# Directional convolutions on 128 partitions in six passes of 12 rows

## What is computed

```
xn = group_norm(x)                                # block 0
feat_h, feat_v      = depthwise 1x7 and 7x1 convolution of xn
feat_d45, feat_d135 = depthwise 7x7 convolution whose only taps are a diagonal
context = mean over pixels of feats**2            # 4 x 96 numbers for an image
attn    = softmax over the 4 directions of (leaky_relu(context @ w_att1.T) @ w_att2.T)
x1 = x + conv3x3(sum_d attn[d] * feats[d], w_proj)
out = x1 + L1(group_norm(x1))                     # block 1: softmax linear attention, a real
                                                  # FFT branch, and one 3x3 convolution
```

## Time and profile before

| | |
|---|---|
| times of three runs | 4177.42, 4215.52, 4221.92 us |
| span of the profiled execution | 4236.6 us |
| TensorE busy | 3960.8 us, 93% |
| VectorE busy | 3033.4 us, 72% |
| ScalarE busy | 1695.8 us, 40% |
| GpSimd busy | 209.5 us, 5% |
| mean DMA traffic | 81 GB/s |

### The profile page before, as it was taken

The page is one execution under the profiler, slowest core; times in us unless marked ns, Lnnn a source line. Parts: engine busy times, 40 slices in busy tenths (PEclk is TensorE's granted clock), DMA queues, the critical chain, the costliest instruction groups (busy, mean ns, idle before and its releaser), DMA issues.

```text
span 4236.6 us, 56479 instructions
## 1 busy us (share of the span) xinstructions
PE 3960.8 (93%) x21202; PEld 3254.3 (77%) x21202; DVE 3033.4 (72%) x2829; ACT 1695.8 (40%) x2912; POOL 209.5 (5%) x376
## 2 busy tenths in 40 slices
PE   4659999999999999999999999999999999999998
PEld 2356879968698687968799686986879687896867
DVE  7988877788677878689777876778886887843020
ACT  3413762247412574127622464215641276203430
POOL 1000000100001000000001000010000000010000
PEclk8879799988799799999999877997999979998779
DMA  4372214712155221822147221552218221350002
GB/s 117 88 177 75 61 41 84 188 51 70 29 133 134 52 69 29 202 73 61 41 97 179 56 61 27 126 143 50 71 26 201 74 63 41 76 137 12 1 3 31
DMA packets 164716, 344.11 MB, mean 81 GB/s; under 512 B 110336, under 2 KB 110576, under 8 KB 164432
## 3 DMA queue, kind: packets, MB, share of 16 engines
q1 hardware_dynamic: 141392, 255.36, 24.5%
q0 software_dynamic: 23040, 84.95, 9.1%
HBM read 189.27 MB, written 150.99 MB: 80 GB/s over the span
## 4 chain that ended last, share of the span: by engine, by line
PE 84%; DVE 9%; ACT 3%; issue 3%; DMA 1%; POOL 0%; SPq 0%; DVEq 0%; ACTq 0%; POOLq 0%
PE banks L936 14%; PE banks L937 14%; PE banks L942 14%; PE banks L961 12%; PE banks L951 6%; PE banks L1003 6%; PE banks L967 5%; DVE feat L702 4%; PE banks L968 4%; PE banks L974 3%; PE banks L1013 3%; DVE e_lo L725 2%; PE banks L990 1%; ACT z L529 1%; DMA feat<-feats_d 1%
## 5 line engine op out<-in xcount | busy, mean ns | idle before, releaser
L702 DVE SCALAR_TENSOR_TENSOR feat<-xin,w,feat 96x1536 f32<-96x1536 f32 x540 | 943.6, 1807 | 28.0 <-ACT feat L488 26.9
L936 PE MATMUL banks<-e_hi,a_hi 96*96 96x384 f32 x1728 | 597.7, 346 | 40.9 <-ACT a_hi L572 40.9
L936 PE MATMUL banks<-e_hi,wp_hi 96*96 96x384 f32 x1728 | 587.7, 341 | 24.2 <-DVE x L780 12.1
L961 PEld LDWEIGHTS banks<-mats,z 96*96 96x96 f32 x3072 | 537.8, 259 | 90.2 <-issue 71.0
L937 PE MATMUL banks<-e_lo,a_hi 96*96 96x384 f32 x1728 | 595.2, 345 | 0.0
L937 PE MATMUL banks<-e_lo,wp_hi 96*96 96x384 f32 x1728 | 586.7, 340 | 0.0
L702 DVE SCALAR_TENSOR_TENSOR feat<-xin,wv,feat 96x1536 f32<-96x1536 f32 x288 | 520.7, 1808 | 79.4 <-ACT feat L488 79.4
L702 DVE SCALAR_TENSOR_TENSOR feat<-xin,wh,feat 96x1536 f32<-96x1536 f32 x288 | 520.6, 1808 | 70.1 <-ACT feat L488 69.2
L961 PE MATMUL banks<-mats,z 96*96 96x96 f32 x3072 | 531.5, 347 | 9.8 <-ACT z L529 9.8
L500 ACT ACTIVATE sqjunk<-feat 96x1536 bf16<-96x1536 f32 x192 | 284.1, 1480 | 228.8 <-DVE feat L702 225.5
L563 ACT ACTIVATE res<-banks 96x768 f32<-96x768 f32 x96 | 77.6, 808 | 727.9 <-PE banks L942 727.9
(11 more groups left out here) (145 smaller groups left out, 5261.1 us busy)
## 6 DMA issues: line engine op xcount, KB each, us to landing
feats_d<-feat SPq DMA_DIRECT2D x160, 576.0 KB, 4.1
feat<-feats_d SPq DMA_DIRECT2D x160, 576.0 KB, 6.5
feat<-in_x SPq DMA_DIRECT2D x48, 576.0 KB, 6.9
res<-in_x POOLq DMA_DIRECT2D x96, 288.0 KB, 4.0
out<-x POOLq DMA_DIRECT2D x96, 288.0 KB, 2.8
out<-res POOLq DMA_DIRECT2D x96, 288.0 KB, 4.4
xin<-in_x SPq DMA_DIRECT2D x32, 792.0 KB, 9.1
xin<-in_x SPq DMA_DIRECT2D x16, 684.0 KB, 10.1
```

The source lines that it names most:

```text
L702: dve.scalar_tensor_tensor(out=dst, in0=src, scalar=taps_w[d](k), in1=dst, op0=ALU.mult, op1=ALU.add).then_inc(tap_done, 1)
L936: pe.matmul(dst, whi[:, t, :], rows(e_hi, a0, n, dx), start=(t == CENTRE_FIRST[0]), stop=False)
L961: last = pe.matmul(ps[0:H, c * W:(c + 1) * W], z[:, :, 4 * g + c], w_dft, start=(c == 0), stop=(c == 3), skip_group_check=True)
```

## The change

- Chunks have 12 rows; `products`, `fg_high`, `fg_low` and the statistics of x run in 8 chunks instead of 6.
- The directional convolutions use all 128 partitions in six passes. Partitions 0 to 95 take chunks 5 to 0, one in each pass. Partitions 96 to 127 take 32 of the 96 channels of chunk 7 in each of passes 0 to 2, and of chunk 6 in passes 3 to 5 (`extra`). The instructions of `taps`, `first_tap` and `square` become 128 x 1152 in place of 96 x 1536, and are as many as before.
- Weights, norm parameters and sums of squares exist in three variants, one for each third of the channels (`wt`, `xpar`, `sqx`, `att1x`). `hidden` has 16 matmul calls in place of 4, of which 12 read 32 rows from partition 96; the group sums of x have 4 calls in place of 1.
- Each pass is loaded with two DMAs and stored with two for each direction (one in pass 5, where chunk 0 stays). Four more loads of x in `start` and eight more loads from `feats_d` for an image.
- The zeroing of edge rows moves from VectorE (`edge_rows`) to ScalarE (`norm_chunk`, one activation with scale 0 in four of the six passes).
- In image 0 `last_direction` has 18 groups of 7 matmul calls with 128 x 128 diagonals (21 of them, made by ScalarE at the start) in place of 24 groups of 7 with 96 x 96. The diagonals lie where `e_hi` and `e_lo` lie later, so GpSimd zeroes the pads only when `last_direction` is done.
- `SUMS_AFTER` becomes (0, 0, 0, 0, 0, 1, 1, 1). Statistics of x go over 24 pieces of 384 in place of 18 of 512.

```
-CR = 16
+LANES = 128
+CR = 12
+PASSES = 6
+VARIANTS = 3
+QUAD = LANES - C
-SUMS_AFTER = (0, 0, 0, 1, 1, 1)
+SUMS_AFTER = (0, 0, 0, 0, 0, 1, 1, 1)
+def extra(q):
+    return q % VARIANTS, NCH - 1 - q // VARIANTS
...
-        xin = sb("xin", [C, 2, XR, XP])
-        feat = sb("feat", [C, DIRS, CR * W])
+        xin = sb("xin", [LANES, 2, XR, XP])
+        feat = sb("feat", [LANES, DIRS, CR * W])
...
+                v, ch = extra(q)
+                lo, hi, at = rows_of(ch)
+                sp.dma_start(xin[C:LANES, q % 2, at:at + hi - lo, PAD:PAD + W],
+                             x[v * QUAD:(v + 1) * QUAD, lo * W:hi * W].rearrange("c (r w) -> c r w", w=W))\
+                    .then_inc(xin_loaded[q % 2], 16)
...
-                        sp.dma_start(feats_d[d, :, ch * CR * W:(ch + 1) * CR * W], feat[:, d]).then_inc(feat_stored[d], 16)
+                        sp.dma_start(feats_d[d, v * QUAD:(v + 1) * QUAD, xch * CR * W:(xch + 1) * CR * W],
+                                     feat[C:LANES, d]).then_inc(feat_stored[d], 16)
+                        if q < PASSES - 1:
+                            sp.dma_start(feats_d[d, :, ch * CR * W:(ch + 1) * CR * W], feat[0:C, d])\
+                                .then_inc(feat_stored[d], 16)
...
                     if not second:
+                        pool.wait_ge(last_dir_sums, VARIANTS * PASSES)
                         zero_pads()
...
+                act.activation(all_rows, all_rows, ACT.Identity, scale=xpar[:, v, 0:1], bias=xpar[:, v, 1:2])\
+                    .then_inc(xin_normed, 1)
+                act.wait_ge(xin_normed, b * (VARIANTS + 1) + min(q, VARIANTS) + 1)
+                act.activation(outside, outside, ACT.Identity, scale=0.0).then_inc(xin_ready, 1)
...
-                                dve.wait_ge(fin_ready, (b - 1) * NG + min(NG, 2 * ch + 3))
+                                dve.wait_ge(fin_ready, (b - 1) * NG + min(NG, (ch + 1) * CR // GR + 1))
...
+                for v in range(VARIANTS):
+                    last = pe.matmul(small_ps[C:LANES, 494 + 2 * v:496 + 2 * v], group[:, v * QUAD:(v + 1) * QUAD], mv[:],
+                                     start=True, stop=True)
...
+                    for v in range(VARIANTS):
+                        for d in range(DIRS):
+                            at = (v * DIRS + d) * MID
+                            last = pe.matmul(small_ps[0:MID, 504:505], att1x[:, at:at + MID], sqx[C:LANES, v, d:d + 1],
+                                             start=False, stop=(v == VARIANTS - 1 and d == DIRS - 1))
```

More of the change, by code:

```diff
@@ L46 @@
 STATS = N // BANK
-XSTAT = CR * W // BANK
+XPIECE = 384
+XSTATS = N // XPIECE
+XSTAT = CR * W // XPIECE
+STORES = 2 * PASSES - 1
 U_MAX = 2 * STATS
@@ L103, in taps_before @@
 def taps_before(b):
-    return 0 if first_image(b) else b * (NCH * TAPS) - NCH * (KT - 1)
+    return 0 if first_image(b) else b * (PASSES * TAPS) - PASSES * (KT - 1)
 def unit_taps(b, u, k, parity):
@@ L116, in firsts_before @@
 def firsts_before(b, q):
[L118 removed]
+    return q * (DIRS - 1) if first_image(b) else b * (DIRS * PASSES) - PASSES + q * DIRS
 def tap_shift(d, k):
@@ L393, in start @@
             def start(b):
-                gn_pow(gnx_small, GN_SMALL, b, 5, 0, gnx_pow)
+                wait(pool, gnx_small, b * GN_SMALL + 5)
+                pool.tensor_tensor(xgp[:, 1], xgp[:, 1], half[:], ALU.pow).then_inc(gnx_pow, 1)
             def step(b, first, second, more):
@@ L441, in _ @@
             pool.wait_ge(consts_set, 5)
+            pool.memset(half[:], -0.5).then_inc(consts_set, 1)
+            pool.wait_ge(consts_set, 6)
             steps(pool, start, step)
@@ L805, in products @@
                 flat = acc[:].rearrange("p r c -> p (r c)")
-                part = feat[:, summed(ch, 0)]
+                part = feat[0:C, summed(ch, 0)]
                 for k in range(k0, k1):
@@ L831, in start @@
             def start(b, between=lambda: None):
-                for n in range(STATS):
+                for n in range(XSTATS):
                     x_stats(b, n, n + 1)
-                    if n % (2 * XSTAT) == 2 * XSTAT - 1 and n + 1 < STATS:
+                    if n % 8 == 7 and n + 1 < XSTATS:
                         between()
@@ L1072, in hidden @@
                     for d in range(DIRS):
-                        last = pe.matmul(small_ps[0:MID, 504:505], att1[:, d, :], l0v[:, d:d + 1], start=(d == 0),
-                                         stop=(d == DIRS - 1))
+                        pe.matmul(small_ps[0:MID, 504:505], att1[:, d, :], l0v[:, d:d + 1], start=(d == 0), stop=False)
+                    for v in range(VARIANTS):
+                        for d in range(DIRS):
+                            at = (v * DIRS + d) * MID
+                            last = pe.matmul(small_ps[0:MID, 504:505], att1x[:, at:at + MID], sqx[C:LANES, v, d:d + 1],
+                                             start=False, stop=(v == VARIANTS - 1 and d == DIRS - 1))
                     last.then_inc(l0_ps, 1)
```

217 lines of the change are left out of this document (120 added, 97 removed).

## The result

The changed kernel takes 4347.7 us (median of 4 runs, 4310.22 to 4358.38), the kernel before 4218.72 us in the same set (4 runs, 4177.42 to 4255.25): a ratio of 1.0324, with an interval of 1.0214 to 1.0433. That is 129 us slower, where 4207 us and no change were forecast. The profiled execution has a span of 4336.8 us with a mean granted clock of 0.867, against 4236.6 us with 0.906.

A forecast was written before the change was run, and what follows sets the result against it. TensorE's work and clock were taken to bound seven of eight rounds. Span 4236.6 - 34 (image 0) + 25 (seven other images) = 4228 us, so a time of about 4207 us; range 4150 to 4262 us.

The forecast's parts named there:

- Taps of image 0 and start: Image 0: 108 shorter VectorE taps save 43 us; later loads at the start cost 1.5 us, `hidden` 2 us.
- rival (5): Taps of image 0: 128 lanes take as long as 96 x 1536 did, the 43 us are gone; 4250 us, chance 0.03.
- Product phase of image 0: Image 0's product phase: eight chunks waiting for their loads take 71.3 us instead of 65.7, so +5.6 us.
- `hidden`: The `a` convolution of the other seven images: 24 more TensorE instructions of `hidden` cost +1.3 us an image.
- rival (3): TensorE: 32-row and 32-column matmuls drain it four times an image, 1.5 us an image; 4217 us, chance 0.10.
- Stall at block 2: The `wp` convolution of seven images: block 2 waits for the later x1_sum(0), 2.5 us an image, between 0 and 7.
- rival (2): The `wp` convolution stalls the full 7 us in seven images, plus 2 to 3 us low clock; 4259 us, chance 0.15.
- The sum of these: Whole kernel: image 0 gains 34 us, the other seven images lose 3.6 us each, 25 us in all.
- rival (4): All eight images: the clock alone can move their sum by 25 us to either side; chance 0.05, in favour.
- the prediction's own bound of 4.9: Seven images: from a loss of 4.9 us an image on, they outweigh the 34 us gained in image 0.
- A count: SyncE queue: 28 more DMA issues for stores and loads of features, taken as having cover.

The follow-up runs named there:

- e9: The changed kernel with each first-pass DFT matmul writing its product twice, 192 columns instead of 96: 4137.7 us, ratio 0.9763.
- e10: The kernel before with each first-pass DFT matmul writing its product twice, 192 columns instead of 96: 4135.96 us, ratio 0.9759.
- e3: The kernel before with ScalarE's unit work placed four uses earlier and nothing added: 4228.59 us, ratio 1.0121.
- e4: The changed kernel plus one ScalarE operation of 0.83 us in the rows stage, on data nobody reads: 4259.78 us, ratio 1.0185.
- e2: The changed kernel without the 12 matmul calls of `hidden` that read 32 rows from partition 96: 4291.28 us, ratio 1.0238.
- e7: The kernel before with the x1 sums as late as the changed kernel has them: 4255.3 us, ratio 1.0142.
- e5: The changed kernel with the same DFT matmuls in a more even order of short and long ones: 4240.19 us, ratio 1.0106.
- e6: The kernel before with the same DFT matmuls in a more even order of short and long ones: 4263.36 us, ratio 1.0205.
- e8: The changed kernel with the even DFT order and four x1 sums between the chunks, one chunk earlier: 4176.26 us, ratio 0.9961.
- e1: The changed kernel with x1_sum(0), (1), (2) each one chunk earlier: 4302.24 us, ratio 1.0246.
- e12: The changed kernel with four x1 sums between the chunks, one chunk earlier, DFT stages as they were: 4272.28 us, ratio 1.0055.
- e11: The changed kernel with doubled columns in the first-pass DFT matmuls and four x1 sums, one chunk earlier: 4103.61 us, ratio 0.9688.

## Why the prediction was wrong

Its terms, one by one:

- *Taps of image 0 and start*, -43.3 + 1.5 + 2 = -39.8 us: measured -38.6: -44.3 from the first tap to the end of the squares, +3.7 for the start (40.58 us instead of 36.89) and +2.0 for `hidden` and what follows it. The start was taken at 1.5 within 0 to 5, and the taps gave 1 us more than forecast. Lanes are free (1.410 us a tap, forecast 1.41), so rival (5) falls. First `maxes` at 352.8 us, forecast 351.
- *Product phase of image 0*: 70.1 us, forecast 71.3. The `wp` convolution there ran longer at the low clock behind a wait of 20.9 us, so the step cost more in the end: -38.6 + 4.4 + 2.2 = -32.0 us, forecast -34.
- *`hidden`*: timeline of TensorE after, around it, in image 1:

```profile
686.73 0.52 PE L1113 MATMUL banks<-l0v,att 96*48 96x1 f32 x8
687.18 1.23 PE L1117 MATMUL banks<-sqx,mats 32*48 32x1 f32 x24
688.35 0.42 PE L972 MATMUL banks<-e_hi,a_hi 96*96 96x384 f32 x1
...
689.65 0.52 PE L972 MATMUL banks<-e_hi,a_hi 96*96 96x384 f32 x1
```

  From 686.73 to 688.35 us, 1.62 us for 32 instructions where 0.44 us went for 8; forecast 1.8. The 24 of them take 1.17 us, 0.049 us each. TensorE drains nowhere that these rows show: the drain at a change of mode, which the Trainium skill states (TensorEngine Tiling (Array Packing), Key Properties), isn't borne out by them, and rival (3) falls. What was left out: a microsecond later the convolution runs at 1.2 GHz for some 3 us (a matmul 0.52 us instead of 0.34). With it, the `a` convolution is 2.5 us longer an image, forecast 1.6.
- *Stall at block 2*: 2.9 us an image, forecast 2.5, and x1_sum(0) 20.3 us behind the copy of block 11, forecast 18 to 21. But the `wp` convolution grew by 5.4 us, since TensorE is at the low clock for 4 to 12 us of it, before 3 to 5. The prediction had priced this in rival (2), for a stall of 7 us, and not for its own of 2.5.
- *The sum of these*: with the clock held up (e9 against e10), after is 34.0 us earlier at the first `maxes` (351.2 against 385.2) and 37.0 us slower over the seven rounds (5.3 us each, forecast 3.6), +3.8 us from profile to profile and +1.7 between the medians, where -9 was forecast. The forecast of this part was 11 to 13 us off, and came that near partly by luck: in e9 against e10 the two convolutions cost 8.7 us an image, forecast 4.1, and the rows, the first DFT stage and the keys and values gave 3.8 us back, forecast at nothing. At 5.3 us an image the rounds outweigh image 0, as the prediction's own bound of 4.9 says.
- *The clock*: the step that failed is rival (4): "it moved single images by 29 us for reasons that the change doesn't touch, so the sum of eight can move by 25 us to either side". Both halves were wrong. It took the eight images for eight draws around one mean, from one profiled execution, in which before had a good order of events in most images: 47.4 us in the second DFT stage five times of seven. The change shifts the stages by a microsecond (inserts in the rows stage take 1.15 and 1.25 us on ScalarE instead of 1.5 and 1.6, and the stage is 17.1 us, not 18.1) and adds instructions and waits in the convolutions, and in its profile nearly every image goes the slow way. Which of these does it isn't shown; e3 has the same microsecond and only part of the loss. But the images of one kernel weren't independent draws: the first DFT stage took 61.4 to 62.2 us in all seven rounds, and the two stages together +96 us, four times the 25. The rows for this were there: two images of the earlier trace rows with 0.97 and 0.86, 29 us apart. Read through to the stage, they would have given the price of the worst case, 8 x 30 us more than all at the high clock. The prediction also named its own falsifier, a mean clock more than 0.02 off 0.91; it was 0.867.
- *A count*: 28 more DMA issues for stores and loads of features were forecast, and it is 32 an image (192 more stores and 64 more loads in the whole).

What stays open: what decides in one image whether the clock falls in a DFT stage and when it comes back. e3 shows that a shift of 1 us lowers it, e4 makes it likely that one can raise it, and e2 and e7 show that neither the added instructions of `hidden` nor the late sums alone are the reason; e5 and e6 only moved the fall from one stage to the other. Executions of one kernel differ too (e8 had 0.871 to 0.931). Why the kernel before comes off better (0.920) than every other version without doubling (0.868 to 0.913) isn't settled either.

## What to carry to other kernels

Where a stage runs at two clocks from image to image, take its time at either level as the bounds for every image, since a shift of a microsecond (e3) can move several of them; and compare versions only within one set, and by level and clock apart, or after the stage holds its clock. TensorE's busy share doesn't show the danger (61.38 of 61.40 us in the slow stage); a stage full of matmuls that take the same time at both clocks was the one in danger here, and for these more columns on the same weights cost next to nothing. When work is cut into more chunks, give every consumer between them (x1_sum(0) to (3)) its own place, and look at what stands behind the last: in e1 the sum left out and the next image's statistics took over the wait of the one that was helped.

## What was not expected of the hardware

- The granted clock fell to 1.2 GHz in stages in which TensorE had work without a gap, and stayed there for some 60 us. The Trainium skill (TensorE: Matmul & The Clock Gate, Part 1) lists 1.2 GHz as the idle state and 2.4 GHz as the busy one. The two levels agree with the rows; that the lower one means an idle engine doesn't, for the profile has it busy for 61.38 of 61.40 us at 0.53.
- Sixteen fp32 matmul instructions of 96 columns on 96 x 96 weights take 2.55 us at 2.4 GHz and 2.60 us at 1.2 GHz. With 192 columns each and the clock up, the group of 3072 is busy for 544.6 us against 536.8, and the kernel's level rises by 18 us (33 from before to e10): twice the streamed columns for nearly nothing, and 2.5% to 3.9% of the kernel's time back from the clock (4240.87 and 4135.96 us, before against e10; 4272.28 and 4103.61 us, e12 against e11).
- A microsecond at the low clock costs 0.28 us here (2370 us for a mean clock lower by 1, of 4200 us in which time at half speed counts half: 2370 / 8400), much the same from the fit and from the single stage.
